# adaLN block with circulant attention and routed experts: the opening stage in another order, its modulation as four rows read back through DRAM

## The reference

```python
mod = (_silu(L0_c) @ L0_wmod).reshape(L0_c.shape[0], 6, 1, -1)      # 4 x 6 x 256
sa, ca, ga, sb, cb, gb = (mod[:, 0], mod[:, 1], mod[:, 2], mod[:, 3], mod[:, 4], mod[:, 5])
ga = (2 * (ga >= 0) - 1) * jnp.maximum(jnp.abs(ga), 0.25)
gb = (2 * (gb >= 0) - 1) * jnp.maximum(jnp.abs(gb), 0.25)
h = _layernorm(x, axis=-1) * (1 + ca) + sa
x = x + ga * _L0_attn_ref(h, Wq, bq, Wk, bk, Wv, bv)
h = _layernorm(x, axis=-1) * (1 + cb) + sb
x = x + gb * _L0_ffn_ref(h, gate_w, dense_1_w, dense_1_b, dense_2_w, dense_2_b)
```

## Time and profile before

| | |
|---|---|
| time before, median of 3 runs | 778.44 us (776.7 to 778.69) |
| the profiled execution | 778.39 us, its span in the trace 776.5 us |
| busy in the span | PE 559.3 (72%), DVE 609.8 (79%), ACT 277.9 (36%), POOL 440.7 (57%) |
| chain that ended last, by engine | PE 47%, DVE 38%, issue 5%, DMA 4%, ACT 2%, POOL 2% |

### The profile page before, as it was taken

How to read it: one execution, slowest core, us unless ns; L and a number is a source line. 1 busy time by engine, 2 the same in 40 slices (tenths; PEclk the granted TensorE clock), 3 DMA queues, 4 the chain that set the end, 5 groups by cost and what they waited for, 6 DMA issues and landing times.

```text
span 776.5 us, 13097 instructions
## 1 busy us (share of the span) xinstructions
PE 559.3 (72%) x3918; PEld 441.1 (57%) x3919; DVE 609.8 (79%) x1209; ACT 277.9 (36%) x422; POOL 440.7 (57%) x256
## 2 busy tenths in 40 slices
PE   4986574848565756512109479999999999999992
PEld 3443343434333434412109458888888888888881
DVE  0266999999999999995599438787888878787873
ACT  1334544444444444413640023333333333333330
POOL 0004645554645555444350326888888888888763
PEclk9978696868686868556555579999999999999997
DMA  8000004142413212123360255787777777777732
GB/s 291 34 1 0 1 19 143 57 133 70 134 66 112 88 43 87 41 81 108 99 154 1 65 141 98 133 140 138 132 141 126 141 128 137 132 136 133 125 49 34
DMA packets 86486, 75.55 MB, mean 97 GB/s; under 512 B 50608, under 2 KB 77744, under 8 KB 86192
## 3 DMA queue, kind: packets, MB, share of 16 engines
q0 software_dynamic: 17472, 30.84, 23.1%
q1 hardware_dynamic: 68976, 44.24, 20.5%
HBM read 41.69 MB, written 23.13 MB: 83 GB/s over the span
## 4 chain that ended last, share of the span: by engine, by line
PE 47%; DVE 38%; issue 5%; DMA 4%; ACT 2%; POOL 2%; SPq 1%; POOLq 0%; DVEq 0%; ACTq 0%
PE ps L520 26%; PE ps L537 13%; PE ps L501 4%; DVE region L856 3%; DVE region L906 3%; DVE region L867 3%; DVE region L796 3%; DVE region L901 3%; DVE region L791 2%; PE ps L386 2%; DVE region L852 2%; PE ps L412 2%; DVE region L861 1%; DVE region L876 1%; DVE region L809 1%
## 5 line engine op out<-in xcount | busy, mean ns | idle before, releaser
L520 PE MATMUL ps<-region,w_sb 128*128 128x256 f16 x1872 | 212.5, 274 | 15.7 <-DMA region<-region 15.7
L520 PEld LDWEIGHTS ps<-region,w_sb 128*128 x1872 | 184.1, 98 | 38.1 <-issue 15.9
L1183 POOL DMA_INDIRECT out_rows<-w_stage,region x78 | 150.6, 1931 | 54.1 <-DVE w_stage L1085 28.7
L1173 POOL DMA_INDIRECT region<-h_scratch,region x78 | 105.0, 1347 | 55.6 <-DVE region L1036 32.1
L1053 DVE TENSOR_SCALAR region<-ps,region 128x256 f32<-128x256 f32 x156 | 67.9, 477 | 71.7 <-PE ps L520 71.7
L412 PE MATMUL ps<-region 128*128 128x512 f32 x192 | 98.4, 676 | 29.8 <-ACT region L606 29.8
L537 PE MATMUL ps<-region 128*128 x936 | 108.6, 273 | 3.6 <-DVE region L1067 3.6
L537 PEld LDWEIGHTS ps<-region 128*128 128x128 f16 x936 | 91.4, 98 | 14.7 <-issue 4.1
L710 ACT ACTIVATE region<-ps,region 128x256 f32<-128x256 f32 x156 | 65.4, 471 | 69.9 <-PE ps L520 69.8
L412 PEld LDWEIGHTS ps<-region 128*128 128x128 f32 x192 | 41.0, 218 | 82.6 <-issue 50.7
L720 ACT ACTIVATE region<-region 128x1024 f16<-128x1024 f32 x39 | 41.2, 1057 | 127.1 <-DVE region L1061 127.1
(11 more groups left out here) (166 smaller groups left out, 858.8 us busy)
## 6 DMA issues: line engine op xcount, KB each, us to landing
w_stage<-in_w SPq DMA_DIRECT2D x24, 512.0 KB, 5.8
region<-in_x SPq DMA_DIRECT2D x8, 512.0 KB, 9.3
out_rows<-region SPq DMA_DIRECT2D x8, 512.0 KB, 3.3
h_scratch<-gb_bc SPq DMA_DIRECT2D x4, 1024.0 KB, 7.5
h_scratch<-region SPq DMA_DIRECT2D x8, 512.0 KB, 3.3
region<-in_wmod SPq DMA_DIRECT2D x1, 1536.0 KB, 9.3
region<-h_scratch,region POOLq DMA_INDIRECT x78, 4.2
region<-region SPq DMA_TRANSPOSE x78, 3.0
```

Source lines behind the costliest of these rows:

```text
L520: mm = pe.matmul(ps[:, GV + 2 * half + a, (f % 2) * MT:(f % 2 + 1) * MT], w, xg_t[:, s, xa * KD + k, :], start=(n == 0), stop=(n == 3 * KD ...
L1173: G.indirect_dma_start(out=xg_rows[:, t % XG, u, :], out_offset=None, in_=h_scratch, in_offset=bass.IndirectOffsetOnAxis(ap=gather_idx[:, ...
L1183: G.indirect_dma_start(out=out, out_offset=bass.IndirectOffsetOnAxis(ap=scatter_idx[:, at:at + 1], axis=0), in_=y_sb[:, t % 2, u, :], in_o ...
```

## The change

- Loads: `wqkv`, the first third of `wmod` (scale and shift), x of block 0, the rest of `wmod`, and the other x blocks on SP's queue; c, the DFT matrix and the constants on ScalarE's, issued ahead of its sigmoid. Each user waits for its own loads.
- TensorE: the scale columns first, then the weights' transform, then block 0's transposes and spectra, then `modulation_rows`: four matmuls with `silu(c)` as the left operand (4 columns), which make ga, sb, cb and gb of the 4 batch entries on 4 partitions, then block 1. `wmod` lies in z's slot 1 to that end.
- ScalarE: block 0's root between the fourth and the fifth copy of the transformed weights; block 1's root before block 0's `spectra`; two copies of modulation rows between block 0's squares and its root of magnitudes.
- VectorE: block 0's rows before block 1's moments; the modulation, on 4 partitions, behind block 1's rows and ahead of `nyquist_units(0)`.
- SP then writes the four rows to the new DRAM table `mod_tab` and reads ga, sb, cb back with a broadcast to all partitions. The gain gb goes from `mod_tab` to `h_scratch`, DRAM to DRAM. The 256 spare rows of the output are filled from x at the start, rather than from `gb_bc` in block 4.
- GpSimd: in each even block `idft_ga` stands behind the products with rq; before, it stood ahead of them.

```diff
     h_scratch = nc.dram_tensor("h_scratch", (TOKENS, ROW), I32).ap()
+    mod_tab = nc.dram_tensor("mod_tab", (BATCH, 4, D), I32).ap()
...
-        gb_bc = sb("gb_bc", [P, BATCH, D])
         gates = sb("gates", [P, TILES, EXPERTS])
...
-        wmod_sb = z_flat[:, 0:KD * 6 * D].rearrange("p (k n) -> p k n", k=KD)
+        wmod_sb = z_flat[:, 6 * BLK:12 * BLK].rearrange("p (k n) -> p k n", k=KD)
+        mod_rows = h2_rows.bitcast(F32).rearrange("p j d -> p (j d)")[0:BATCH, :].rearrange("b (m d) -> b m d", m=4)
-        silu_rep = p_flat[:, 0:KD * BATCH * P].rearrange("p (k b m) -> p k b m", k=KD, b=BATCH)
...
-            sp.dma_start(c_sb, c_t).then_inc(const_in, 16)
-            sp.dma_start(dft_sb, dft[:, :, 0:NF]).then_inc(const_in, 16)
-            sp.dma_start(alt_rep, tri[:, 3, :]).then_inc(const_in, 16)
-            sp.dma_start(bq_sb, bqkv).then_inc(const_in, 16)
-            sp.dma_start(ident_sb[:], ident).then_inc(const_in, 16)
-            sp.dma_start(idft_sb, idft).then_inc(const_in, 16)
-            sp.dma_start(gate_sb, gate_w).then_inc(const_in, 16)
-            sp.dma_start(tri_sb, tri[:, 0:2, :]).then_inc(const_in, 16)
             sp.dma_start(wraw, wqkv).then_inc(wraw_in, 16)
-            sp.dma_start(wmod_sb, wmod).then_inc(wmod_in, 16)
-            for t in range(XS):
+            sp.dma_start(wmod_sb[:, :, 0:2 * D], wmod[:, :, 0:2 * D]).then_inc(sca_in, 16)
+            sp.dma_start(x_sb[:, 0], x_blk[0]).then_inc(x_in[0], 16)
+            sp.dma_start(wmod_sb[:, :, 2 * D:6 * D], wmod[:, :, 2 * D:6 * D]).then_inc(wmod_in, 16)
+            for t in range(1, XS):
                 sp.dma_start(x_sb[:, t], x_blk[t]).then_inc(x_in[t], 16)
+            sp.dma_start(out[TOKENS:OUT_ROWS, :], x[0:OUT_ROWS - TOKENS, :]).then_inc(spare_out, 16)
             for n in range(2):
                 load_weights(sp, n)
+            sp.wait_ge(mod_ready, 6)
+            sp.dma_start(mod_tab, mod_rows.bitcast(I32)).then_inc(mod_out, 16)
+            sp.wait_ge(mod_out, 16)
+            sp.dma_start(mod_bc.bitcast(I32), mod_tab[:, 0:3, :].partition_broadcast(P)).then_inc(mod_in, 16)
             for t in range(NBLK):
...
                 if t < BATCH:
-                    sp.wait_ge(mod_ready, 9)
-                    gain = gb_bc[:, t, :].bitcast(I32).unsqueeze(1).to_broadcast([P, SEQ // P, D])
+                    gain = mod_tab[t, 3, :].partition_broadcast(P).unsqueeze(1).to_broadcast([P, SEQ // P, D])
                     sp.dma_start(hs_gb[t], gain).then_inc(gb_out, 16)
-                if t == BATCH:
-                    sp.dma_start(out[TOKENS:OUT_ROWS, :].rearrange("(u p) d -> p u d", p=P), gb_bc[:, 0:SUB, :]).then_inc(spare_out, 16)
                 if t + XS < NBLK:
...
-                pe.wait_ge(const_in, 128)
-                pe.wait_ge(wraw_in, 16)
+                pe.wait_ge(wraw_in, 32)
                 for c in range(3):
...
                         mm.then_inc(pe_setup, 1)
+                pe.wait_ge(bq_in, 32)
                 for r in range(3):
...
                 mm.then_inc(pe_setup, 1)
-                pe.wait_ge(wmod_in, 16)
+            def scale_columns():
+                pe.wait_ge(sca_in, 16)
                 pe.wait_ge(silu_done, 1)
...
                                            start=(ke == 0), stop=(ke == KD - 1))
-                mm.then_inc(pe_setup, 1)
-            def broadcast_modulation():
-                pe.wait_ge(rep_done, 1)
-                for b in range(BATCH):
-                    for half in range(2):
-                        n = 2 * b + half
-                        pe.wait_ge(act_setup, n + 1)
-                        for ke in range(KD):
-                            mm = pe.matmul(ps[:, n, :], silu_rep[:, ke, b, :],
-                                           wmod_sb[:, ke, (2 + 2 * half) * D:(4 + 2 * half) * D],
-                                           start=(ke == 0), stop=(ke == KD - 1))
-                        mm.then_inc(mod_mm, 1)
-                pe.wait_ge(mod_copied, 2 * BATCH)
+                mm.then_inc(sca_mm, 1)
+            def modulation_rows():
+                pe.wait_ge(wmod_in, 16)
+                for half in range(2):
+                    for ke in range(KD):
+                        mm = pe.matmul(ps[0:BATCH, OUT + half, :], c_silu[:, ke, :],
+                                       wmod_sb[:, ke, (2 + 2 * half) * D:(4 + 2 * half) * D],
+                                       start=(ke == 0), stop=(ke == KD - 1))
+                    mm.then_inc(mod_mm, 1)
...
                 pe.wait_ge(n_ready, TPB * (t + 1))
+                if t == 0:
+                    pe.wait_ge(ident_in, 16)
+                    pe.wait_ge(act_setup, 7)
+                    pe.wait_ge(sca_copied, 1)
                 if t >= 1:
...
+                if t == 0:
+                    pe.wait_ge(const_in, 48)
                 pe.wait_ge(ny_kvd, t + 1)
...
                 pe.wait_ge(ga_ready, t // 2 + 1)
+                if t == 0:
+                    pe.wait_ge(mod_copied, 2)
                 if t >= 1:
...
+            scale_columns()
             transform_weights()
-            broadcast_modulation()
             for t in range(-1, NBLK + 2):
...
                     project(t + 1)
+                if t == -1:
+                    modulation_rows()
                 if t >= 2:
...
-            act.wait_ge(const_in, 128)
+            nc.scalar.dma_start(c_sb, c_t).then_inc(c_in, 16)
+            nc.scalar.dma_start(dft_sb, dft[:, :, 0:NF]).then_inc(wraw_in, 16)
+            nc.scalar.dma_start(ident_sb[:], ident).then_inc(ident_in, 16)
+            nc.scalar.dma_start(alt_rep, tri[:, 3, :]).then_inc(bq_in, 16)
+            nc.scalar.dma_start(bq_sb, bqkv).then_inc(bq_in, 16)
+            nc.scalar.dma_start(idft_sb, idft).then_inc(const_in, 16)
+            nc.scalar.dma_start(gate_sb, gate_w).then_inc(const_in, 16)
+            nc.scalar.dma_start(tri_sb, tri[:, 0:2, :]).then_inc(const_in, 16)
+            act.wait_ge(c_in, 16)
             nc.scalar.activation(c_sig, c_sb, ACT.Sigmoid).then_inc(sig_done, 1)
-            for n in range(6):
-                act.wait_ge(pe_setup, n + 1)
-                nc.scalar.activation(w_spec[:, n // KD, n % KD, :], ps[:, n, 0:NF], ACT.Copy).then_inc(act_setup, 1)
-            act.wait_ge(pe_setup, 7)
-            nc.scalar.activation(bias_f, ps[:, 6, 0:9], ACT.Copy).then_inc(act_setup, 1)
-            act.wait_ge(pe_setup, 8)
-            nc.scalar.activation(sca_t.rearrange("p w k b -> p (w k b)"), ps[:, 7, 0:4 * BATCH],
-                                 ACT.Copy).then_inc(act_setup, 1)
-            for b in range(BATCH):
-                act.wait_ge(mod_mm, 2 * b + 1)
...
+            def weights_in():
+                act.wait_ge(sca_mm, 1)
+                nc.scalar.activation(sca_t.rearrange("p w k b -> p (w k b)"), ps[:, 7, 0:4 * BATCH],
+                                     ACT.Copy).then_inc(sca_copied, 1)
+                for n in range(6):
+                    act.wait_ge(pe_setup, n + 1)
+                    nc.scalar.activation(w_spec[:, n // KD, n % KD, :], ps[:, n, 0:NF], ACT.Copy).then_inc(act_setup, 1)
+                    if n == 3:
+                        project(0)
+                act.wait_ge(pe_setup, 7)
+                nc.scalar.activation(bias_f, ps[:, 6, 0:9], ACT.Copy).then_inc(act_setup, 1)
+            def modulation_rows():
+                for half in range(2):
+                    act.wait_ge(mod_mm, half + 1)
+                    nc.scalar.activation(mod_rows[:, 2 * half:2 * half + 2, :],
+                                         ps[0:BATCH, OUT + half, :].rearrange("b (m d) -> b m d", m=2),
+                                         ACT.Copy).then_inc(mod_copied, 1)
...
                 if t == 0:
-                    act.wait_ge(mod_ready, 1)
+                    act.wait_ge(sca_ready, 1)
                 for k in range(KD):
...
             def evacuate(t):
+                if t == 1:
+                    act.wait_ge(mod_copied, 2)
                 if t >= 2:
...
                 act.wait_ge(h2_ready, TPB * (t + 1))
+                if t == 0:
+                    act.wait_ge(mod_out, 16)
                 if t >= 1:
...
-            project(0)
+            weights_in()
             project(1)
...
                     squares(t + 1)
+                if t == -1:
+                    modulation_rows()
                 if t >= 2:
...
             dve.wait_ge(silu_done, 1)
-            V.tensor_copy(silu_rep, c_silu.unsqueeze(3).to_broadcast([P, KD, BATCH, P])).then_inc(rep_done, 1)
-            V.tensor_copy(ident_h[:], ident_sb[:]).then_inc(gate_split, 1)
...
-            dve.wait_ge(act_setup, 8)
-            V.tensor_scalar(sca_t[:, 1], sca_t[:, 1], 1.0, None, ALU.add).then_inc(mod_ready, 1)
-            def clamp_gain(g, n):
+            def gate_parts():
+                dve.wait_ge(ident_in, 16)
+                dve.wait_ge(const_in, 48)
```

(61 more changed lines are left out.)

13 lines of the change are left out of this document (1 added, 12 removed).

## The result

The changed kernel takes 802.25 us (median of 4 runs, 800.62 to 803.75), the kernel before 777.70 (4 runs, 776.70 to 778.69): a ratio of 1.032, 95% interval 1.0294 to 1.0347. It is slower; the prediction had said 764.0 with 758.0 to 769.5, and faster with a chance of 0.95. The span of the profiled execution grew from 776.5 to 801.1 us.

The account below looks back on a forecast made before the run. VectorE was taken to bound the kernel after the first bind, a chain of loads and stages the opening before it. Terms -18.1 - 1.0 + 2.5 + 2.2 = -14.4 took 778.4 to 764.0 us, range 758.0 to 769.5.

Parts of the forecast that it names:

- the second half of part 4: Four gain transfers of 1 MB reading DRAM instead of SBUF: 3.7 us free, cost 0; if 5 us longer, 5.2 in all.
- The rival held 769.2 at 0.16: Opening loads come no earlier (769.4), or the DRAM gain transfers hold the weights (769.2); chance 0.16.
- The rival "Slower": Table broadcast to all partitions takes 30 us or more, GpSimd holds its products, VectorE waits: 780.9 us; chance 0.03.
- the signs of being wrong: First matmul after 12, GpSimd waiting for the table, or ScalarE waiting several us for weight chunks in the first four blocks.
- Part 1: Opening: TensorE starts earlier, at 8.9, first transposes at 22.0, spectra copy at 24.3; gain 18.1 us (16.5 to 19.7).
- Part 2: First spectra matmuls: start cold again, perhaps for a shorter time; 1.0 us gained, bounds 0 and 3.0.
- Part 3: Modulation behind the first spectra, held by GpSimd's magnitudes, Nyquist behind it: first bind 2.5 us late (1.6 to 4.2).
- Part 4, the first half: Modulation written to DRAM and broadcast back, landing at 78.7 with 3.8 us slack before GpSimd needs it: cost 0.
- Part 5: idft_ga behind the rq products: eight scans held 0.4 each, 1.0 saved at the old place; loss 2.2 us.
- The sum: All parts together: -18.1 - 1.0 + 2.5 + 2.2 = -14.4 us, giving 764.0.

Follow-up runs that it names:

- The Nyquist experiment: nyquist_units(0) put ahead of the modulation, against the kernel with gains from SBUF and idft_ga back ahead of the rq products in blocks 2, 4, 6: 757.28 us.

## Why the prediction was wrong

**The step that failed** is the second half of part 4, the four gain transfers: "So 3.7 us are free: 0. If a gain transfer took 5 us longer, 1.3 per block, 5.2 in all." The mechanism was named, with its queue, its victims and its slack, but both its price and its rank were off. The transfers went from 7.2 (from SBUF, in the same frame) to 19.8, 12.6 longer instead of 0 with a bound of 5; VectorE waited 52.3, and 39.7 us net came of it. Put through the prediction's own working, 12.6 less the 3.7 that are free makes 8.9 per block and 35.6 in all, so the slack was about right and the time of the transfer was the term that failed. I priced a DRAM source by no row at all. The nearest rows, the broadcast of 1 MB in 8.6, read each row 128 times, and the experiments show that 128 reads cost nothing; 1024 was outside what any row of the trace bounded, and a bound of 5 us was a guess that stood as if it were one. The rival held 769.2 at 0.16, so the range, too, ended 33 us short. The rival "Slower", at 0.03, had the direction but another transfer: its broadcast of the table landed in 6.1 and held nobody. Of the signs of being wrong the last came true, ScalarE's wait for weight chunks (54.0 us in four waits).

**Part 1, right.** Landing forecast at 8.9 (7.3 to 10.5): 7.64, first matmul 7.69. The cold small matmuls, forecast at 3.2: 3.57. The transposes, forecast at 22.0, started at 20.74 and the `spectra` copy (L606, now L622), forecast at 24.3, at 22.76; as said, it was held by block 1's root behind block 1's moments. Gain 19.65 instead of 18.1.

**Part 2, not shown.** 13.11 for 24 records against 13.51; a gain of 0.4 instead of 1.0, with a mean granted clock of 0.80 over the stage, where before it was 0.78. The same matmuls took 12.26 to 13.48 in the profiles of the eleven kernels with this opening, so 0.4 can't be told from that spread.

**Part 3, right.** Forecast: the modulation held until the magnitudes end, bind 2.5 behind the root's usual place. Its first operation starts at 43.22 and lasts 1.48, to 0.3 behind the end of GpSimd's 3.42 from 41.00, where a like one later takes 0.41 (that GpSimd held it is read from these times; no run moved the one without the other); the root ended at 45.94 and bind began at 47.95, 2.0 later. The Nyquist experiment shows that 1.16 of this was the place behind it.

**Part 4, the first half, right.** The modulation is written at 46.90, the table read at 48.92 and back by 55.0, long before GpSimd's products with rq end at 59.65. GpSimd never waits for it.

**Part 5, right.** Net loss 2.2 forecast. With gains from SBUF the stretch from the first bind to the routing's matmuls is 344.8 us against 342.7 before (66.1 to 408.8): 2.1. The scans before, of which the even blocks have the shortest (1.22 and 1.20 us):

```profile
L873 DVE TENSOR_TENSOR_SCAN region<-region x8: 1224/1254/1285, 79.0 to 337.4; 128x512 f32<-128x512 f32 x8
...
L876 DVE TENSOR_TENSOR_SCAN region<-region x8: 1198/1230/1260, 80.1 to 338.6; 128x512 f32<-128x512 f32 x8
```

In the same even blocks they now take 1.54 and 1.59, so 0.32 and 0.39 longer, close to the 0.4 each of the sum: 2.8 in four blocks instead of 3.2. One reading was off: before, the product was 1.01 in two of the four even blocks (2 and 6), not in three; in block 4 `idft_ga` ended at 213.82, before that product began at 214.40. So 0.6 was saved instead of 1.0, and 2.8 - 0.6 is the forecast 2.2: two small errors that cancel.

**The sum.** Without the four slow transfers the parts give about what was added up: 764.0 forecast, that is 14.4 gained; 762.59 and 760.91 measured in the two kernels that cure only them, 14.1 and 16.8 gained on their own chips.

## What to carry to other kernels

A broadcast from DRAM isn't one case: ask how often each row is read. Up to 128 times was free here, 1024 times cost 11 to 13 us per MB, and eight copies of each row (32 KB for the four) cured it. An estimate, not tried: at the 70 GB/s of the window above, one read of 1 KB takes 15 ns, so 512 reads of a row would take 7.5 us, about as long as the transfer takes anyway, and two or three copies might do. Before a source moves from SBUF to DRAM, look for a row with the same number of reads, or bound the price as widely as the ignorance is, and let a transfer that nobody needs soon stand behind those that somebody does: there the same slow one cost nothing.

## What was not expected of the hardware

One row of 1 KB read 1024 times: 19.8 us to DRAM and 18.3 to SBUF, 70 GB/s with the DMA engines 0.97 busy; 8, 128 or 1024 rows for the same 1 MB: 8.4 to 8.6 us. Scans with two SBUF inputs wait for GpSimd like products do (1.54 and 1.59 instead of 1.22 and 1.20 beside two operations of 256 columns; the longer times go when these move away). And the time at which TensorE's clock rises from 1.2 to 2.4 GHz differs from run to run enough to move the opening: over the eleven profiled kernels with this opening the transform of the weights took 6.84 to 8.46 us and the first spectra 12.26 to 13.48, at a mean granted clock between 24 and 37 us of 0.87 in the shortest and 0.74 in the longest. Five of them, the changed kernel among these, don't differ at all before the first gain transfer and still took 7.43 to 8.45 for the transform.
